# Sorted token rows for the experts: transposed by VectorE in 32x32 blocks instead of by TensorE, with gate/up weights laid out to match

## What is computed

```python
x  = L0_attn_x                                  # (1, 1024, 256)
xn = layernorm(x)
out = x + attention(xn) + ffn(xn)

# attention: q, k, v = xn @ w_qkv, phi = elu + 1, a decaying causal scan
#   s_t = decay * s_{t-1} + k_t * v_t   and   z_t = decay * z_{t-1} + k_t
#   out = (q * s / clip(sum(q * z), 1e-6)) @ w_out

def ffn(x):                                     # 8 experts, one per token, F = 512
    logits = x @ router_w.T
    gate, e = sigmoid(max(logits)), argmax(logits)
    xs = x * gate
    routed = (silu(xs @ w_gate[e]) * (xs @ w_up[e])) @ w_down[e]
    shared = (silu(x @ s_gate) * (x @ s_up)) @ s_down
    return routed + shared
```

## Time and profile of the kernel before

| | |
|---|---|
| median of 3 runs | 129.22 us (129.17 to 129.29) |
| the profiled execution | 129.24 us |
| its span on the profile | 127.6 us |
| TensorE busy with matmuls | 122.1 us, 96% |
| VectorE busy | 79.4 us, 62% |
| ScalarE busy | 53.4 us, 42% |
| GpSimd busy | 35.4 us, 28% |
| DMA traffic | 15748 packets, 25.02 MB |

### The profile page before, as it was taken

How to read it: one execution, slowest core, us unless ns; L and a number is a source line. 1 busy time by engine, 2 the same in 40 slices (tenths; PEclk the granted TensorE clock), 3 DMA queues, 4 the chain that set the end, 5 groups by cost and what they waited for, 6 DMA issues and landing times.

```text
span 127.6 us, 2426 instructions
## 1 busy us (share of the span) xinstructions
PE 122.1 (96%) x822; PEld 106.1 (83%) x822; DVE 79.4 (62%) x175; ACT 53.4 (42%) x113; POOL 35.4 (28%) x65
## 2 busy tenths in 40 slices
PE   4989999999999999999999999999999999999990
PEld 1248776788888857999999999999999978999990
DVE  0799695997899999875575553505040428922471
ACT  1678796829987546322222222242221337200000
POOL 7804040003879300040303030303030301687500
PEclk9999999999999999999999999999999999999999
DMA  3784999999993210129797989888982031033437
GB/s 83 207 281 37 330 360 244 181 207 397 385 380 136 82 51 0 46 81 318 264 321 258 295 275 277 307 280 303 281 303 63 9 86 51 13 89 104 112 101 244
DMA packets 15748, 25.02 MB, mean 196 GB/s; under 512 B 1296, under 2 KB 12632, under 8 KB 15736
## 3 DMA queue, kind: packets, MB, share of 16 engines
q1 hardware_dynamic: 13368, 20.66, 53.1%
q0 software_dynamic: 1456, 3.41, 8.2%
q10 hardware_dynamic: 912, 0.80, 1.9%
HBM read 18.78 MB, written 6.08 MB: 195 GB/s over the span
## 4 chain that ended last, share of the span: by engine, by line
PE 80%; POOL 6%; issue 5%; DMA 4%; DVE 2%; ACT 0%; DVEq 0%; POOLq 0%
PE ps L1112 25%; PE ps L1126 13%; PE ps L300 6%; POOL q_sb L458 6%; PE ps L302 5%; PE ps L301 5%; PE ps L975 5%; PE ps L988 4%; PE ps L981 4%; PE ps L1066 4%; DMA q_sb<-sorted_rows,slot_row 2%; PE ps L1053 2%; DMA sorted_rows<-yrow 2%; PE ps L1060 2%; DVE x_sb L895 1%
## 5 line engine op out<-in xcount | busy, mean ns | idle before, releaser
L1112 PE MATMUL ps<-xgT,gu 128*128 128x144 f32 x256 | 34.2, 287 | 0.0
L1112 PEld LDWEIGHTS ps<-xgT,gu 128*128 128x128 f32 x256 | 32.3, 190 | 0.5 <-issue 0.2
L826 DVE TENSOR_TENSOR wqkv<-rz,ps 128x288 f32<-128x288 f32 x16 | 7.3, 454 | 25.5 <-ACT rz L576 25.5
L440 POOL DMA_DIRECT2D sorted_rows<-yrow x9 | 5.0, 558 | 54.7 <-DVE yrow L821 54.7
L1126 PE MATMUL ps<-wqkv,dn 128*128 128x144 f32 x128 | 17.4, 289 | 0.0
L576 ACT ACTIVATE rz<-ps 128x288 f32<-128x288 f32 x16 | 6.5, 409 | 25.0 <-PE ps L1112 25.0
L1126 PEld LDWEIGHTS ps<-wqkv,dn 128*128 128x128 f32 x128 | 16.1, 190 | 0.0
L432 POOL DMA_INDIRECT sorted_rows<-xn,slot_row x8 | 9.8, 1220 | 15.4 <-ACT xn L514 13.6
L300 PE MATMUL ps<-xT_hi,sgu_hi 128*128 128x512 f32 x32 | 13.0, 407 | 0.0
L301 PE MATMUL ps<-xT_lo,sgu_hi 128*128 128x512 f32 x32 | 12.6, 394 | 0.0
L302 PE MATMUL ps<-xT_hi,sgu_lo 128*128 128x512 f32 x32 | 12.6, 394 | 0.0
(11 more groups left out here) (162 smaller groups left out, 231.3 us busy)
## 6 DMA issues: line engine op xcount, KB each, us to landing
gu<-in_L_ffn_w_gate_up_dram SPq DMA_DIRECT2D x8, 1024.0 KB
dn<-in_L_ffn_w_down_dram SPq DMA_DIRECT2D x8, 512.0 KB
sorted_rows<-zeros SPq DMA_DIRECT2D x1, 2592.0 KB, 18.0
wqkv<-sorted_rows SPq DMA_DIRECT2D x10, 144.0 KB
sorted_rows<-yrow POOLq DMA_DIRECT2D x9, 128.0 KB, 2.1
sgu<-_ffn_shared_gate_up_dram SPq DMA_DIRECT2D x1, 1024.0 KB, 6.2
wqkv<-in_L_attn_w_qkv_dram SPq DMA_DIRECT2D x3, 256.0 KB, 3.7
x_sb<-in_L_attn_x_dram SPq DMA_DIRECT2D x2, 256.0 KB, 3.6
```

Of the source, the lines that this page charges most:

```text
L826: V.tensor_tensor(hr[:, 2 * h:2 * h + 2, :].rearrange("p f s -> p (f s)"), act_sb[:, h, 0:2 * SLOTS], ps[:, 2 * h + 1, 0:2 * SLOTS], ALU.m ...
L1112: ins = mm(ps[:, 2 * h + u, (f % 2) * SLOTS:(f % 2 + 1) * SLOTS], gu[p][:, kc, col:col + P], xgT[:, kc, :], start=(kc == 0), stop=(kc == K ...
```

## The change

The four TensorE transposes of a tile and the ScalarE copy behind them go. VectorE's `transpose`, which turns each 32x32 block in place, writes `xgT` directly. So that block-wise transposes are enough, the rows are loaded in blocks: partition block q (32 partitions) gets features 64q to 64q+63 of every row, 160 rows (5 groups of 32) instead of 144. That makes 4 DMAs of 32 partitions x 5 x 64 elements (256 bytes) for a tile, where there was one. Feature 2p + c now lands on partition p in chunk c, and the gate/up weights are loaded with the same layout (`"e (p c) n"`, so both rows of a partition lie side by side in DRAM: 8 KB).

In the expert tile VectorE now does: product of half 0, wait for the rows of the next tile and for the end of gate/up half 1, transpose, product of half 1, `rows_copy`. TensorE's `transpose_back` moves from between the halves to after half 1. SP's next load of rows waits for VectorE's transpose. The first tile's transpose stands on VectorE ahead of `hidden(6)`.

```diff
-    ROWS = (TILES + 3) * SLOTS
+    ROWS = (TILES + 2) * SLOTS + NSQ * SQ            # SQ = 32, NSQ = 5
-        xgT = sb("xgT", [P, KC, SLOTS], F32)
+        xgT = sb("xgT", [P, KC, NSQ * SQ], F32)
-        xg = early[0:HS, 0:2 * D].rearrange("p (j d) -> p j d", j=2)
+        xg = early[:, 0:NSQ * SQ * KC].rearrange("p (j f) -> p j f", j=NSQ)
-        gu_dram = w_gate_up.rearrange("e (c p) n -> e p c n", p=P)
+        gu_dram = w_gate_up.rearrange("e (p c) n -> e p c n", c=KC)
# SP
-            def sorted_load(t):
-                sp.dma_start(xg, sorted_rows[bass.ds(t * SLOTS + SLOTS, SLOTS), :].rearrange("(j p) d -> p j d", p=HS)).then_inc(s_xg, 16)
+            def sorted_load(first, s_load):
+                for q in range(P // SQ):
+                    rows = sorted_rows[bass.ds(first, NSQ * SQ), q * SQ * KC:(q + 1) * SQ * KC]
+                    sp.dma_start(xg[q * SQ:(q + 1) * SQ, :, :], rows.rearrange("(j p) f -> p j f", p=SQ)).then_inc(s_load, 16)
@@ rows_of
-                    sp.wait_ge(s_xgT, t + 2)
-                    sorted_load(t + 2)
+                    sp.wait_ge(s_xgc, t + 2)
+                    sorted_load(t * SLOTS + 3 * SLOTS, s_xg)
# ScalarE
-            def sorted_copy(done, bank):
-                act.wait_ge(s_xgT, done)
-                A(xgT[:, :, :], ps[:, bank, 0:KC * SLOTS].rearrange("p (c s) -> p c s", c=KC), ACT.Copy).then_inc(s_xgc, 1)
-                if k == LAST - 1:
-                    sorted_copy(1, 7)
@@ expert_tile
-                sorted_copy(t + 2, 4)
# VectorE
+            def sorted_in():
+                V.transpose(xgT[:, :, :], xg.rearrange("p j (f c) -> p c j f", c=KC)).then_inc(s_xgc, 1)
             for k in range(LAST):
+                if k == LAST - 1:
+                    dve.wait_ge(s_xg0, 64)
+                    sorted_in()
                 hidden(k)
@@ expert_tile
                     if h == 0:
-                        rows_copy(t, b, stored)
+                        dve.wait_ge(s_xg, 64 * t + 64)
+                        dve.wait_ge(s_gup, 2 * t + 2)
+                        sorted_in()
+                rows_copy(t, b, stored)
# TensorE
-                    if (k, u, kc) == (LAST - 1, 1, 1):
-                        transpose_sorted(7, s_xg0, 16)
-            def transpose_sorted(bank, s_load, loaded):
-                ...
@@ expert loop
-                                             gu[p][:, kc, col:col + P], xgT[:, kc, :], start=(kc == 0), stop=(kc == KC - 1))
+                                             gu[p][:, kc, col:col + P], xgT[:, kc, 0:SLOTS], start=(kc == 0), stop=(kc == KC - 1))
                         ins.then_inc(s_gup, 1)
-                        if h == 0:
-                            pe.wait_ge(s_yrow, t + 1)
-                            transpose_back(t + 1)
+                    pe.wait_ge(s_yrow, t + 1)
+                    transpose_back(t + 1)
                     if e == 0:
                         pe.wait_ge(s_sh, LAST)
-                    transpose_sorted(4, s_xg, 16 * t + 16)
```

More of the change, by code:

```diff
@@ L19 @@
 SLOTS = 144
-HS = SLOTS // 2
+SQ = 32
+NSQ = (SLOTS + SQ - 1) // SQ
 REST = SLOTS - 128
@@ L260, in build @@
         s_xg = sem("s_xg")
-        s_xgT = sem("s_xgT")
         s_xgc = sem("s_xgc")
@@ L359, in _ @@
             sp.wait_ge(s_wlq, 1)
-            sp.dma_start(xg, sorted_rows[SLOTS:2 * SLOTS, :].rearrange("(j p) d -> p j d", p=HS)).then_inc(s_xg0, 16)
+            sorted_load(SLOTS, s_xg0)
             sp.wait_ge(s_plan, 1)
-            sp.wait_ge(s_xgT, 1)
-            sp.dma_start(xg, sorted_rows[2 * SLOTS:3 * SLOTS, :].rearrange("(j p) d -> p j d", p=HS)).then_inc(s_xg, 16)
+            sp.wait_ge(s_xgc, 1)
+            sorted_load(2 * SLOTS, s_xg)
             for e in range(E - 2):
@@ L368, in _ @@
                 rows_of(e)
-            sp.wait_ge(s_xg, 16 * ends[7] + 16)
+            sp.wait_ge(s_xg, 64 * ends[7] + 64)
             sp.wait_ge(s_lastrest, 1)
```

## The result

The changed kernel takes 133.25 us (median of 4 runs, 132.25 to 134.12), the kernel before 129.19: a ratio of 1.031, 95% interval 1.022 to 1.041. Run again later beside other kernels it gave 1.019 (1.017 to 1.021), 131.50 against 128.98. So it is slower by 2 to 3%, where I had forecast a gain of 0.5%. The profiled execution took 132.44 us, its span is 130.8.

A forecast was written before the change was run, and what follows sets the result against it. TensorE, 96% busy, was taken to bound the kernel: 129.24 - 2.2 (transposes) + 1.5 (first tile's stall) = 128.5, with 0.1 us for losses at tile seams 128.6 us, or -0.5%; range 127.9 to 130.6.

The forecast's parts named there:

- TensorE's transposes, -2.2 us: Expert tiles: removing TensorE's four transposes saves 0.28 us in each of eight tiles, -2.2 us.
- The length of VectorE's transpose, 0.50 us: VectorE: the new transpose of 320 elements a partition takes 0.50 us, bounds 0.40 to 0.60.
- Within the tile it cost nothing: Expert tile: with VectorE's transpose ahead, half 1's product is in time for down by about 0.1 us; cost nothing.
- The stall ahead of the first tile, +1.5 us: First tile: VectorE's transpose queues behind other work, gate/up starts at 52.16 instead of 50.65, +1.5 us.
- The refill of `gu` is covered by 1.7 us: SP's queue: gate/up refill issued 1.4 us later, landing 4.0 us after issue; of 3.4 us slack 1.7 remain.
- A packet's cost, "a third of the way, which still fits": DMA engines, row loads: 640 packets of 256 bytes add +0.05 to +1.3 us a tile; taken +0.5, which fits.
- theory D: From the experiments: the DMA engines have no room for a 6.2 us tile with the refill, whatever the order.
- Rival B: Expert tiles: at 43 ns a packet DMA needs 6.9 us a tile, refills slip, TensorE waits; 131.1 us, chance 10%.
- A: Expert tiles: VectorE's transpose is slow, 0.78 us, and sets the tile; 130.3 us, chance 17%.
- C: First tile: no stall because VectorE gets there earlier, so the whole gain stays; 126.7 us, chance 6%.
- D: First tile: TensorE's clock falls to 1.2 GHz in the stall ahead of it; +6 us, 134.6 us, chance 4%.

The follow-up runs named there:

- a_split: Changed kernel with the first tile's VectorE transpose two steps earlier and two of four row loads on ScalarE's queue; 126.53 us, 0.981 of before.
- a_split_late: Changed kernel with two of four row loads on ScalarE's queue, first transpose where the change put it; 128.77 us, 0.997 of before.
- b_late: Kernel before with the gate/up refill issued 1.2 us later, after the end of the down projection; 129.06 us, 1.002 of before.
- after_again: Changed kernel measured once more, unedited; 131.50 us, 1.019 of before.
- a_thin: Changed kernel, first transpose two steps earlier, second to fourth row loads from the third tile on cut to 32 of 160 rows; 128.95 us, 0.998 of before.
- a_gu4k: Changed kernel, first transpose two steps earlier, each gate/up refill issued as two DMAs of 4 KB pieces; 131.71 us, 1.020 of before.
- a_act: Changed kernel with all four row loads of tile t + 2 issued from ScalarE's queue instead of SP's; 131.62 us, 1.020 of before.
- a_one: Changed kernel, first transpose two steps earlier, three of four row loads left out from the third tile on; 126.52 us, 0.981 of before.

## Why the prediction was wrong, step by step

- **TensorE's transposes, -2.2 us: right.** Tiles that nothing holds up follow each other in 6.21 us, 0.30 less than before, where I took 0.28.
- **The length of VectorE's transpose, 0.50 us: right.** It is 511 ns. The estimate by the Trainium skill's figure (VectorE: DVE Perf Modes, The three transpose paths) was 0.60; the trace is 0.09 below it and on the line through my two rows. Within the tile it cost nothing, as reasoned: the product of half 1 starts at 63.26 and down goes through without a gap.
- **The stall ahead of the first tile, +1.5 us: right.** The first tile starts at 52.32, forecast 52.16, behind a wait of 1.98 us. The pair of a_split and a_split_late puts the whole price at 2.0 to 2.2 us.
- **The refill of `gu` is covered by 1.7 us: wrong, and it is the step that failed.** Two of its terms were off. The issue was put 1.4 us later; it came 1.8 later relative to half 1 (the first row load 0.2 us later than forecast, and three more at 0.5 us each, not 0.44). And the landing was put 4.0 us after issue, by adding the bytes of four windows until they made 1049 KB. Those bytes were not all `gu`: by the packet records (b_late above) 948 KB were, and the other 200 KB rows and `dn`. That alone is 0.3 us. What counted is the last tenth: some packets of the refill came much later than the rest, and the last of them ended 6.9 us after issue. So the room in the kernel before was between nothing and 1.4 us, next to none at this tile, and not 3.4; the median landings in the other runs are 5.2 (b_late) to 7.1 us (after_again). A later issue alone was still free (b_late), because the last packet did not come later by it; with 640 small packets between, and 1.8 us of delay, it was not.
- **A packet's cost, "a third of the way, which still fits": wrong in the conclusion.** The packet records give 18 ns for one of 256 bytes and 46 ns for one of 1 KB (medians), so a tile's rows cost each of 16 engines 0.7 us instead of 0.4: +0.3, where I took +0.5. The sum of busy time did fit, as theory D's fall shows. But the refill behind these packets lands later (6.3 against 5.6 us with 384 fewer), and a_thin puts 1.3 us on the packets in all. Why they delay it by more than their own time, no run separates. The rule of the Trainium skill (DMA: Bandwidth & Descriptors, Specifications) that transfers under 512 bytes don't reach line rate spoke in this direction; the trace agrees in that 256 bytes take 18 ns where 1 KB takes 46, and no run here shows where the threshold lies.
- **Rival B** named the mechanism, refills that slip until TensorE waits for `gu`, with 131.1 and a chance of 10%. Its time was near the two measurements (131.5 and 133.3) partly by luck: it laid the slip to the engines' capacity at 43 ns a packet, which the 18 ns rule out, where SP's issue time carries the larger part.
- **A and C** did not happen. **D** did not happen where I looked for it: the granted clock stayed at 1.00 through the 2 us stall ahead of the first tile. But the waits for `gu` can bring it about. In a_gu4k's profile it fell to 0.50 after 3 us without work and cost some 2.9 us, half of the 6 that I had put on it; the changed kernel's two executions of 134.1 us, with a mean clock of 0.986 and 0.982, look like the same, which no trace shows. The Trainium skill (TensorE: Matmul & The Clock Gate, the section on the HAM clock gate) says that idleness brings the lower clock back; a_gu4k's trace agrees.

## What to carry to other kernels

Before a DMA is cut into several, look at what is issued behind it on the same queue, and how late that may come: here 1 MB of weights paid for four small loads. Don't take a transfer's landing from the bytes that all queues move: nine tenths of this one had started 4.2 us after issue, and the last packet ended at 6.9. Take a measured landing, or when its last packet ends. A run in which only the issue is delayed doesn't measure the room, since the end need not move with the issue. When small loads must be many, try them split over two queues: here all on the other queue let the large one run first and made the small ones late, and half and half made neither wait.

## What the runs showed that I had not expected

- Small loads issued right behind a large one, on another queue, suffered more than it did: the 40 KB row loads landed in 2.1 us ahead of the refill and in 3.9 us beside it (a_act), while the refill took 5.4 there, no more than in a_one (5.6), where three of the four loads are gone. Issued half and half (a_split) they took 2.4 and 2.3.
- A refill issued 1.27 us later had its last packet at the same time, 69.58 against 69.64.
- TensorE transposes whose input is read at every second column load their weights in 207 ns instead of 141.
